# Tile 1's row numbers on their own, the largest expert as tile 10, and b2 added by rows outside the tiles

## The chip, the core and the metric

The kernel runs on one core of one Trainium2 chip. The metric is device time in microseconds of one execution, as the median of several. Times "at 320" are counted from the start of the profiled execution's span.

## The reference

The input is a table x of 625 rows (tokens) by 512, with 20,000 edges. Four residual layers follow one another: a graph convolution, a small feed-forward layer on a few features, a three-layer graph network, and last a tree-routed mixture of 16 experts. Only the last one is touched here. In short:

```
leaf = 4 binary decisions of a router on the normed rows      # one of 16 experts for each row
for each expert (w1 512x2048, b1, w2 2048x512, b2), m = (leaf == expert):
    h = gelu(xn @ w1 + b1)
    out += m * (h @ w2 + b2)
result = x + out
```

All weights are float32: 4 MB for w1 and 4 MB for w2 of each expert. With these inputs the largest expert has 73 rows, the others 16 to 54, 625 in all.

## The kernel before

The layers ahead of the experts run until about 290 us. The rows before the last layer (x3) are then stored into `out`, and their normed form into a table `normed_rows` in DRAM; both in five chunks of 125 rows.

The expert layer works by tiles. A tile is up to 64 rows of one expert (SA), and one tile, called "more" in the code, has 32 further rows (SB_) for the expert with the most rows. Tiles go in pairs: tile i = 2p + b uses buffer b of w1_sb, w2_sb, xT, y_sb. There are 16 tiles here (the pair count `last` is 7, read from the device). Experts 0, 1 and 2 are always tiles 0, 1 and 2, so that their weights can be fetched before the router has run; the largest of the other experts is exchanged with whichever expert would stand at tile `last2`, the first of the last pair (tile 14 here).

For one tile, TensorE (PE) multiplies the turned rows by w1 into two PSUM banks (32 matmuls, `first_a`, L952), turns each bank (L969), adds a product of a one-hot column with the b2 rows (2 matmuls of 256 columns by two halves, L986: this starts the accumulation), turns the rows of the next tile (`turn_rows`, L908), and multiplies the gelu of the hidden rows by w2 (64 matmuls, `second_a`, L1000). The more-tile adds `first_b` (L961) and `second_b` (L1012) for its 32 further rows. DVE copies banks (L1392), turned rows (L1318) and the tile's bias column (L1394); ScalarE does gelu (L629) and copies the result to y_sb (L641).

GpSimd moves rows by indirect DMA on the software queue: `gather` brings the rows of a tile from normed_rows into x_row (L458), `scatter` adds a tile's result to `out` (L466), both with row numbers that `pick` copies (L452). A number that stands for an empty slot is over the bound and is skipped. In its loop GpSimd, for tile i, waits until the rows of tile i+1 are turned, gathers tile i+2, scatters tile i, and waits until that has landed. There is one x_row, so a gather can't start before the rows ahead of it are turned. Ahead of the loop it gathers tile 1 and the more-tile's 32 rows.

The order of the start: tile 0's rows don't come by gather but by a product of a selector with the normed rows (L914, L1314). The row numbers of all tiles after it are worked out in `number_rows` on DVE (L1364 to L1384) during tile 0, with a product on PE in its midst (`slot_tokens`, L927). Only then (s_idx) does GpSimd gather tile 1. PE turns tile 1's rows after tile 0's last product.

SyncE (SP) issues the weight loads, 2 MB each (two halves of w1, L378, and two of w2, L386), on the hardware queue, in a fixed order: w1 of tile 4 once tile 0 has used its buffer, w2 of tile 2, w1 of tile 3, w2 of tile 3, w2 of tile 4, w1 of tile 5, w2 of tile 5, and then w1 and w2 of tile i+2 with tile i. Each half waits for PE to have used the same half of that buffer (s_w1u, s_h, s_l2). The first 16 MB are fetched long before.

Of the kernel before, what the change touches and what calls it, by code (L numbers as in the profile page):

```python
# [62 lines left out]
FIXED = 3  # L63
MORE = (N_NODES - 1) // SA
# [6 lines left out]
def build(nc, x, src, dst, Wconv, bconv, Wlin, blin, Wa, ba, Ws, bs, Wg, bg, Wr, br, W1, b1, W2, b2, out):  # L71
    ctx = ExitStack()
    with ctx:
# [117 lines left out]
        row_inB = row_inB[0:2 * SB_, :]  # L191
        half_ofB = maps[:, 950:951]
# [5 lines left out]

        b1T = FB[:, 1536:1536 + NE * (MH + 1)].rearrange("p (e m) -> p e m", e=NE)
        b1T_flat = FB[:, 1536:1536 + NE * (MH + 1)]  # L200
        bT = [FB[:, 1824 + b * (MH + 1):1824 + (b + 1) * (MH + 1)] for b in range(2)]

        w1_two = [G[:, 0:HID]] + [a[:, :, :].rearrange("p c n -> p (c n)")[:, 0:HID] for a in (C, xs, xn)]
        b2_rows = FB[:, 1900:1900 + DIM]
# [4 lines left out]
        def sv(at, *dims):  # L209
# [35 lines left out]
        s_sel = sem("tile0_selector_ready")  # L245
# [5 lines left out]
        s_b2, s_b1, s_b1T, s_b1Tc = (sem(n) for n in  # L251
            ("b2_in", "b1_in", "b1_transposed", "b1_copied"))
        s_b2z, s_xst, s_ost, s_slots, s_rows, s_idx = (sem(n) for n in
            ("b2_cleared", "normed_stored", "x3_stored", "slots_ready", "slot_rows", "row_numbers"))
        s_peh = sem("pe_held")
# [7 lines left out]
        s_xTB, s_xTBc, s_hB, s_hBc, s_hTB, s_geluB, s_l2B = (sem(n) for n in ("more_transposed",  # L263
            "more_copied", "more_hidden", "more_hidden_copied", "more_hidden_transposed", "more_gelu", "more_out"))
# [14 lines left out]
        def _(sp):  # L279
# [69 lines left out]
            sp.wait_ge(s_b2z, 1)  # L349
            sp.dma_start(b2_rows[0:NE, :], b2).then_inc(s_b2, 16)  # L350
# [52 lines left out]
        def _(pool):  # L403
# [34 lines left out]
            pool.wait_ge(s_gh, NCH * 3)  # L438
            nc.gpsimd.memset(b2_rows, 0.0).then_inc(s_b2z, 1)
            pool.sem_inc(s_yfree, 2)  # L440
            pool.wait_ge(s_xst, 16 * 2 * NCH)
            pool.wait_ge(s_table, 1)
            last = pool.value_load(npairs_t[0:1, 0:1], min_val=NE // 2 - 1, max_val=MAX_PAIRS - 1)
            pool.wait_ge(s_idx, 3)

# [23 lines left out]

            pool.wait_ge(s_xT, 1)  # L470
            gather(1, 1)
            pick(row_inB, 2, 2 * last, 2)
# [4 lines left out]
            pool.wait_ge(s_ost, 16 * 2 * NCH)  # L477
            with pool.Fori(0, last) as p:
                for b in range(2):
                    i = 2 * p + b  # L480
                    hold(s_xT, i + 2)
                    gather(i + 2, 2 * i + 3)
                    scatter(i, b, 2 * i + 4)
                    hold(s_yst[b], 16 * p + 16)
                    pool.sem_inc(s_yfree, 1)
            scatter(2 * last, 0, 4 * last + 3)
            pick(row_outB, 1, 2 * last, 4 * last + 4)
            pool.wait_ge(s_ycpB, 1)
            nc.gpsimd.indirect_dma_start(out=out.rearrange("t (g n) -> (t g) n", g=4),
                                         out_offset=bass.IndirectOffsetOnAxis(ap=row_outB, axis=0), in_=y_sbB, in_offset=None,  # L490
                                         bounds_check=4 * N_NODES - 1, oob_is_err=False, compute_op=ALU.add).then_inc(s_ystB, 16)
            scatter(2 * last + 1, 1, 4 * last + 5)
# [6 lines left out]
        def _(act):  # L499
# [120 lines left out]
            def tile_out(p, b, end=False):  # L620

                i = 2 * p + b
                more = end and b == 0
# [18 lines left out]
                if more:  # L642
                    act.wait_ge(s_l2B, 1)
                    nc.scalar.activation(y_sbB, P[:, 5, 0:128], ACT.Copy).then_inc(s_ycpB, 1)

            with act.Fori(0, last) as p:
                for b in range(2):
                    tile_out(p, b)
            for b in range(2):
                tile_out(last, b, end=True)  # L650
# [3 lines left out]
        def _(pe):  # L654
# [264 lines left out]
            pe.wait_ge(s_b2z, 1)  # L919
            pe.wait_ge(s_b2, 16)  # L920
# [10 lines left out]
            def tile(p, b, end=False):  # L931

                i = 2 * p + b
                more = end and b == 0
# [7 lines left out]
                def first_ready(j):  # L942
                    if not usual:
                        pe.wait_ge(s_w1_two, 16 * KD)
                    elif b or isinstance(p, int):
                        pe.wait_ge(s_w1[b][j], 16 * (p + 1))
                    else:
                        pe.wait_ge(s_w1[b][j], 16 * p)

                def first_a(h, k):  # L950
# [3 lines left out]
                    if k == KD - 1:  # L954
                        mm.then_inc(s_h, 1)
                    elif h == 1 and k == 1:
                        mm.then_inc(s_w1u, 1)

                def first_b(k):
# [3 lines left out]
                    if k == KD - 1:  # L963
                        mm.then_inc(s_hB, 1)

# [5 lines left out]

                for j in range(2):
                    first_ready(j)
                    for h in range(2):
                        for k in (2 * j, 2 * j + 1):
                            first_a(h, k)
                if more:
                    pe.wait_ge(s_xTBc, 1)
                    for k in range(KD):
                        first_b(k)  # L980
# [13 lines left out]
                def second_a(q):  # L994
# [3 lines left out]
                    for m in range(4 * q, 4 * q + 4):  # L998
                        for g in range(2):
                            mm = nc.tensor.matmul(P[g * SA:(g + 1) * SA, 7, 0:256], hT[:, m, :], w2_sb[b][:, m, g * 256:(g + 1) * 256],  # L1000
                                                  start=False, stop=(m == MH - 1))
                    mm.then_inc(s_l2, 1)

                def second_b(q):
                    pe.wait_ge(s_geluB, q + 1)
                    if q == 0:
                        for g in range(4):
                            nc.tensor.matmul(P[g * SB_:(g + 1) * SB_, 5, 0:128], bT[b][:, MH:MH + 1].to_broadcast([128, SB_]),
                                             b2_rows[:, g * 128:(g + 1) * 128], start=True, stop=False)
                    for m in range(4 * q, 4 * q + 4):  # L1010
                        for g in range(4):
                            mm = nc.tensor.matmul(P[g * SB_:(g + 1) * SB_, 5, 0:128], hTB[:, m, :], w2_sb[b][:, m, g * 128:(g + 1) * 128],  # L1012
                                                  start=False, stop=(m == MH - 1))
                    return mm

                second_a(0)
                if more:
                    pe.wait_ge(s_hBc, 1)
                    turn(0, 2).then_inc(s_hTB, 1)
                for q in range(1, 4):  # L1020
# [6 lines left out]
                if more:  # L1027
                    for q in range(4):
                        mm = second_b(q)
                    mm.then_inc(s_l2B, 1)  # L1030
# [6 lines left out]
            with pe.Fori(2, last) as p:  # L1037
# [3 lines left out]
            pe.wait_ge(s_hc, 4 * last)  # L1041
            pe.sem_inc(s_peh, 1)
# [4 lines left out]
            for b in range(2):  # L1047
                tile(last, b, end=True)

        @block.vector  # L1050
        def _(dve):
# [212 lines left out]
            for d in range(4):  # L1264
# [16 lines left out]
            more, last2, tmp = small[:, 744:750], small[:, 750:751], small[:, 752:756]  # L1281
            ts(thr[:, :], iota[:, 0:16], float(SA), None, ALU.mult)
            rank, not0, rank0 = sv(0, NCH, NE), sv(90, NCH), sv(100, NCH)
            link(ts(not0[0:NC, :], leaf[0:NC, :, 0], -EMPTY, EMPTY, ALU.mult, ALU.add))
# [3 lines left out]
            link(tt(rank0[0:NC, :], rank[0:NC, :, 0], not0[0:NC, :], ALU.add))  # L1288
            tt(sel[0:NC], iota[0:NC, 0:SA].unsqueeze(1).to_broadcast([NC, NCH, SA]),
               rank0[0:NC, :].unsqueeze(2).to_broadcast([NC, NCH, SA]), ALU.is_equal).then_inc(s_sel, 1)  # L1290
# [25 lines left out]
            def copy_inputs(i, b):  # L1316
# [9 lines left out]
            link(ts(last2, more[:, 5:6], 2.0, float(NE - 2), ALU.mult, ALU.add))  # L1326
            copy_inputs(0, 0)
            link(tt(top[:, :], big[:, :], iota[:, 0:NE], ALU.mult))
# [8 lines left out]
            link(ts(at2, iota[:, 0:TAB + 2], last2, None, ALU.is_equal))  # L1337
            ts(one, iota[:, 0:TAB + 2], tmp[:, 0:1], None, ALU.is_equal)
            link(tt(row, eid, at2, ALU.mult))
            link(nc.vector.tensor_reduce(tmp[:, 1:2], row, AX.X, ALU.add))  # L1340

            link(tt(one, one, at2, ALU.subtract))
            tt(tmp[:, 2:3], tmp[:, 1:2], tmp[:, 0:1], ALU.subtract)
            link(tt(tmp[:, 3:4], last2, tmp[:, 0:1], ALU.subtract))
            link(stt(pos, one, tmp[:, 3:4], iota[:, 0:TAB + 2], ALU.mult, ALU.add))
            link(stt(eidf, one, tmp[:, 2:3], eid, ALU.mult, ALU.add))
# [8 lines left out]
            nc.vector.tensor_copy(b1T[:, :, 0:MH].rearrange("p e (q r) -> p e q r", r=8),  # L1355
                                  P[:, 5, 0:256].rearrange("p (r e q) -> p e q r", r=8, q=2))
            nc.vector.tensor_copy(b1T[:, :, MH], ident[:, 0:NE]).then_inc(s_b1Tc, 1)
# [28 lines left out]
            def tile_copies(p, b, end=False):  # L1386
# [3 lines left out]
                for t in range(2):  # L1390
                    dve.wait_ge(s_h, 2 * i + t + 1)
                    nc.vector.tensor_copy(h_sb[:, t, :].rearrange("p (r n) -> p r n", r=4), P[:, t, :].rearrange("p (n r) -> p r n", r=4)).then_inc(s_hc, 1)  # L1392
                    if t == 0:
                        nc.vector.tensor_copy(bT[b], b1T_flat[:, bass.ds(e * (MH + 1), MH + 1)]).then_inc(s_bTc, 1)  # L1394
                if end and b == 0:
# [4 lines left out]
                if not (end and b):  # L1400
# [36 lines left out]
```

## Time and profile before

| what | value |
|---|---|
| median of 3 runs | 613.92 us (612.63 to 615.91) |
| the profiled execution | 611.82 us, span 609.9 us |
| PE busy | 532.0 us (87%) |
| DVE, ScalarE, GpSimd busy | 191.5, 160.8, 62.4 us |
| moved by DMA | 145.71 MB, of which hardware queue 142.91 |
| granted TensorE clock, mean | 0.983 |

PE is TensorE's matmuls, PEld its weight loads, ACT ScalarE, POOL GpSimd, SP the engine that issues the weight loads. A group of the profile names the line, engine, operation, output<-input, and at its end, behind the bar, busy time and mean ns of one, and then the idle time before it with what ended most of it. "DMA to landing" is the time from the issue instruction's start to the last byte.

### The profile page before, as it was taken

How to read it: one execution, taken by the hardware profiler on the slowest of the kernel's cores; microseconds unless marked ns; L12 is line 12 of the kernel's file. 1: busy time of each engine (PE TensorE's matmuls, PEld its weight loads, DVE VectorE, ACT ScalarE, POOL GpSimd, SP SyncE). 2: the span in 40 equal slices, each digit the busy share in tenths (PEclk: the TensorE clock that was granted, in tenths of full speed). 3: DMA queues.
4: the chain of work that ended last, by engine and by line, in shares of the span. 5: the costliest groups of instructions: out<-in, count | busy, mean ns of one | idle time of the engine just before them, and what ended most of it. 6: DMA issues, size and time to landing. Idle time of an engine off the chain costs nothing.

```text
span 609.9 us, 9957 instructions
## 1 busy us (share of the span) xinstructions
PE 532.0 (87%) x3090; PEld 284.6 (47%) x3090; DVE 191.5 (31%) x600; ACT 160.8 (26%) x548; POOL 62.4 (10%) x88
## 2 busy tenths in 40 slices
PE   1967878889899999999895999999998778878994
PEld 1534555544356657444451555555543344334463
DVE  5997777482520010146740101111111001100100
ACT  1667778202011101002120222222222022202311
POOL 3000000021000000000012221221112120212021
PEclk9979999999999999999897999999999999999998
DMA  6169900100202010024686979999999999999980
GB/s 122 13 223 429 429 21 5 30 0 0 87 1 70 0 36 33 0 89 140 226 352 253 420 304 423 421 426 421 424 425 420 422 428 425 421 422 432 418 338 7
DMA packets 25209, 145.71 MB, mean 239 GB/s; under 512 B 10335, under 2 KB 12585, under 8 KB 16738
## 3 DMA queue, kind: packets, MB, share of 16 engines
q1 hardware_dynamic: 21986, 142.91, 57.9%
q0 software_dynamic: 3200, 2.50, 2.0%
q8 instruction: 14, 0.23, 0.1%
q14 instruction: 9, 0.07, 0.0%
HBM read 142.38 MB, written 4.72 MB: 241 GB/s over the span
## 4 chain that ended last, share of the span: by engine, by line
PE 58%; DMA 20%; DVE 8%; ACT 6%; issue 5%; ACTq 2%; POOL 0%; DVEq 0%; SPq 0%; POOLq 0%
DMA w<-in_L_ffn_W 18%; PE P L952 13%; PE P L1000 11%; PE P L839 8%; PE P L849 7%; PE P L858 4%; ACT H L537 2%; PE P L693 2%; ACT H L543 2%; PE P L969 2%; DVE stats L1134 2%; DMA XT<-normed_rows,C 1%; PE P L986 1%; PE P L802 1%; PE P L801 1%
## 5 line engine op out<-in xcount | busy, mean ns | idle before, releaser
L952 PE MATMUL P<-w,H 128*64 128x512 f32 x480 | 108.6, 600 | 17.1 <-DMA w<-in_L_ffn_W 15.8
L1000 PE MATMUL P<-w,FB 128*64 128x256 f32 x1024 | 115.6, 381 | 5.5 <-DMA w<-in_L_ffn_W 5.5
L629 ACT ACTIVATE FB<-P,FB 128x64 f32<-128x64 f32 x256 | 54.3, 362 | 156.2 <-PE P L969 156.2
L1000 PEld LDWEIGHTS P<-w,FB 128*64 128x64 f32 x1024 | 72.0, 137 | 43.9 <-issue 10.7
L1392 DVE COPY H<-P 128x512 f32<-128x512 f32 x32 | 22.1, 692 | 215.2 <-PE P L952 215.2
L693 PE MATMUL P<-H 125*125 125x500 bf16 x176 | 59.6, 414 | 18.5 <-ACT H L543 18.0
L952 PEld LDWEIGHTS P<-w,H 128*64 128x64 f32 x480 | 35.9, 138 | 81.6 <-issue 60.5
L1116 DVE TENSOR_SCALAR H<-iota,small 125x626 bf16<-125x626 f16 x176 | 60.2, 382 | 14.0 <-issue 8.9
L839 PE MATMUL P<-G,XT 128*125 128x512 f32 x120 | 52.0, 592 | 0.0
L693 PEld LDWEIGHTS P<-H 125*125 125x125 bf16 x176 | 25.1, 143 | 44.5 <-ACT H L543 30.9
L849 PE MATMUL P<-C,H 125*128 125x313 f32 (+1 forms) x160 | 42.4, 425 | 0.0
L694 PE MATMUL P<-H 125*125 125x127 bf16 x176 | 40.0, 227 | 0.0
L1234 DVE TENSOR_SCALAR H<-P,dis_c 125x512 f32<-125x512 f32 x15 | 11.3, 751 | 83.8 <-PE P L839 83.8
L537 ACT ACTIVATE H<-iota,small 125x126 bf16<-125x126 f16 x88 | 30.4, 392 | 23.6 <-issue 15.0
L849 PEld LDWEIGHTS P<-C,H 125*128 125x128 f32 x160 | 30.2, 189 | 12.5 <-issue 1.0
L839 PEld LDWEIGHTS P<-G,XT 128*125 128x125 f32 x120 | 22.4, 187 | 27.9 <-issue 27.6
L466 POOL DMA_INDIRECT out<-XT,C x16 | 25.6, 1602 | 79.8 <-ACT XT L641 78.7
L543 ACT ACTIVATE H<-H,ones 125x126 bf16<-125x126 bf16 x88 | 30.6, 392 | 5.4
L641 ACT ACTIVATE XT<-P 128x256 f32<-128x256 f32 x16 | 6.2, 384 | 87.2 <-PE P L1000 87.2
L452 POOL COPY C<-C 128x1 int32 (+2 forms) x33 | 7.4, 225 | 194.4 <-DMA out<-XT,C 130.0
L605 ACT ACTIVATE XT<-P,bg_c 128x313 f32<-128x313 f32 (+1 forms) x16 | 8.4, 523 | 67.9 <-PE P L849 67.9
L694 PEld LDWEIGHTS P<-H 125*125 125x125 bf16 x176 | 25.6, 145 | 0.0
(294 smaller groups left out, 441.9 us busy)
## 6 DMA issues: line engine op xcount, KB each, us to landing
w<-in_L_ffn_W SPq DMA_DIRECT2D x62, 2048.0 KB, 28.7
G<-in_L_gnn_W SPq DMA_DIRECT2D x3, 1024.0 KB, 5.3
xs<-in_x SPq DMA_DIRECT2D x1, 1120.0 KB
out<-xs SPq DMA_DIRECT2D x5, 224.0 KB
normed_rows<-xn SPq DMA_DIRECT2D x5, 224.0 KB
G<-in_L_ffn_W SPq DMA_DIRECT2D x1, 1024.0 KB, 5.0
C<-in_L_ffn_W SPq DMA_DIRECT2D x1, 1024.0 KB, 5.3
xs<-in_L_ffn_W SPq DMA_DIRECT2D x1, 1024.0 KB, 7.3
```

What stands on the lines that cost most here:

```text
L466: nc.gpsimd.indirect_dma_start(out=out.rearrange("t (g n) -> (t g) n", g=2), out_offset=bass.IndirectOffsetOnAxis(ap=row_out[b], axis=0), ...
L537: near = nc.scalar.activation(sqd[0:NC, j, :], iota[0:NC, even:even + DW], ACT.Square, bias=ef[0:NC, 1, j, bass.ds(lo_g + u, 1)], scale=-1.0)
L543: nc.scalar.activation(D[0:NC, j, :], sqd[0:NC, j, :], ACT.Relu, bias=ones[0:NC, 0:1], scale=-1.0).then_inc(s_dhot, 1)
L629: g = nc.scalar.activation(hT[:, m, :], P[:, 3 + rd, c * SA:(c + 1) * SA], ACT.Gelu, bias=bT[b][:, m:m + 1])
L693: nc.tensor.matmul(P[0:NC, b0, 0:GROUP], hot, S[0:NC, j, 0:GROUP], start=False, stop=False, skip_group_check=True)
L694: nc.tensor.matmul(P[0:NC, b0 + 1, 0:LAST], hot, S[0:NC, j, GROUP:GROUP + LAST], start=False, stop=False, skip_group_check=True).then_inc( ...
L839: mm = nc.tensor.matmul(P[0:NC, c, :], XTn[:, k, c * NC:(c + 1) * NC], Gw[:, k, :], start=(k == 0), stop=(k == KD - 1))
L849: mm = nc.tensor.matmul(P[:, (5 + g) % 8, 0:b - a], Hn[0:NC, c, m * 128:(m + 1) * 128], C[0:NC, c, a:b], start=(c == 0), stop=(c == NCH - 1))
L858: mm = nc.tensor.matmul(P[0:NC, (5 + t) % 8, :], C[0:NC, c, t * NC:(t + 1) * NC], Hn[0:NC, c, :], start=(c == 0), stop=(c == NCH - 1))
L952: mm = nc.tensor.matmul(P[g * SA:(g + 1) * SA, h, :], xT[b][:, k, :], w1a[k][:, h, g], start=(k == 0), stop=(k == KD - 1))
L1000: mm = nc.tensor.matmul(P[g * SA:(g + 1) * SA, 7, 0:256], hT[:, m, :], w2_sb[b][:, m, g * 256:(g + 1) * 256], start=False, stop=(m == MH - 1))
L1116: hot = ts(S[0:NC, j, 0:NPAD], iota[0:NC, :], ef[0:NC, 0, j, bass.ds(lo_g + u, 1)], None, ALU.is_equal)
```

## The change

- DVE makes a selector for tile 1 (in `slots`) beside that of tile 0, and PE multiplies it with the token numbers (10 matmuls of one column). DVE turns that into tile 1's row numbers (`row_one`), which GpSimd uses for tile 1's gather without the numbers of all tiles. PE turns tile 1's rows before the last quarter of tile 0's second product.
- DVE also works out each token's expert (`expert_of`). GpSimd gathers, in five chunks of 125 tokens, that expert's row of b2, and adds these rows to `out` by five indirect DMAs. It waits for all five ahead of its loop over tiles.
- The load of the 16 rows of b2, its clearing, the one-hot column in the bias table and the products L986 (and those of the more-tile, L1008) go. The second product starts its own accumulation.
- The more-tile is tile 10 always (LARGE), not the first of the last pair. Its `first_b` is interleaved with `first_a`, and `second_b` with `second_a`; what releases its weight buffers is the last user of each part. The loops of all engines are split around tile 10.

```diff
+            link(tt(rank01[0:NC], rank[0:NC, :, 0:2], not01[0:NC], ALU.add))
...
+            tt(slots[0:NC], iota[0:NC, 0:SA].unsqueeze(1).to_broadcast([NC, NCH, SA]),
+               rank01[0:NC, :, 1:2].to_broadcast([NC, NCH, SA]), ALU.is_equal).then_inc(s_selx, 1)
+            link(tt(val[0:NC], leaf[0:NC], iota[0:NC, 0:NE].unsqueeze(1).to_broadcast([NC, NCH, NE]), ALU.mult))
+            link(nc.vector.tensor_reduce(not01.rearrange("p c t -> p (c t)")[0:NC, 0:NCH], val[0:NC], AX.X, ALU.add))
+            ts(row_of[0:NC, :], token[0:NC, :], -1.0, None, ALU.add)
+            nc.vector.tensor_copy(expert_of[0:NC, :], not01.rearrange("p c t -> p (c t)")[0:NC, 0:NCH]).then_inc(s_eid, 1)
...
+            dve.wait_ge(s_row1, 1)
+            v = P[:, 5, 384:385]
+            link(ts(row_one_f, v, 0.5, EMPTY, ALU.is_lt, ALU.mult))
+            link(stt(row_one_f, v, 2.0, row_one_f, ALU.mult, ALU.add))
+            tt(row_one, row_one_f, half_of, ALU.add).then_inc(s_idx1, 1)
```

GpSimd, ahead of its loop:

```diff
-            pool.wait_ge(s_xst, 16 * 2 * NCH)
-            pool.wait_ge(s_table, 1)
-            last = pool.value_load(...)
-            pool.wait_ge(s_idx, 3)
...
+            pool.wait_ge(s_ost, 16 * 2 * NCH)
+            pool.wait_ge(s_eid, 1)
+            for c in range(NCH):
+                nc.gpsimd.indirect_dma_start(out=b2_tok[c][0:NC, :], out_offset=None, in_=b2,
+                                             in_offset=bass.IndirectOffsetOnAxis(ap=expert_of[0:NC, c:c + 1], axis=0),
+                                             bounds_check=NE - 1, oob_is_err=False).then_inc(s_b2, 16)
+            pool.wait_ge(s_xst, 16 * 2 * NCH)
+            pool.wait_ge(s_xT, 1)
+            pool.wait_ge(s_idx1, 1)
+            nc.gpsimd.indirect_dma_start(out=x_row, ..., ap=row_one, ...).then_inc(s_xr, 16)
+            pool.wait_ge(s_b2, 16 * NCH)
+            for c in range(NCH):
+                nc.gpsimd.indirect_dma_start(out=out, out_offset=bass.IndirectOffsetOnAxis(ap=row_of[0:NC, c:c + 1], axis=0),
+                                             in_=b2_tok[c][0:NC, :], in_offset=None,
+                                             bounds_check=N_NODES - 1, oob_is_err=False, compute_op=ALU.add).then_inc(s_b2st, 16)
+            pool.wait_ge(s_table, 1)
+            last = pool.value_load(...)
+            pool.wait_ge(s_idx, 3)
+            pick(row_inB, 2, LARGE, 1)
+            pool.wait_ge(s_rowB, 1)
             nc.gpsimd.indirect_dma_start(out=x_rowB, ...).then_inc(s_xrB, 16)
+            pick(row_outB, 1, LARGE, 2)
+            pool.wait_ge(s_b2st, 16 * NCH)
+            pool.sem_inc(s_yfree, 1)
             ... loop: hold(s_xT, i + 2); gather(i + 2); scatter(i); hold(s_yst[b], 16 * p + 16)
```

PE, in a tile:

```diff
-                pe.wait_ge(s_bTc, i + 1)
-                pe.wait_ge(s_ycp, i + 1)
-                for g in range(2):
-                    nc.tensor.matmul(P[g * SA:(g + 1) * SA, 7, 0:256], bT[b][:, MH:MH + 1].to_broadcast([128, SA]),
-                                     b2_rows[:, g * 256:(g + 1) * 256], start=True, stop=False)
-                if not (first or end and b):
+                if not (first or end):
                     pe.wait_ge(s_xr, 16 * i + 16)
                     turn_rows(i + 1)
...
                 for q in range(1, 4):
                     if first and q == 2:
                         slot_tokens()
+                    if first and q == 3:
+                        pe.wait_ge(s_xr, 16)
+                        turn_rows(1)
                     second_a(q)
-                if first:
-                    pe.wait_ge(s_xr, 16)
-                    turn_rows(1)
```

## Rows read from the trace of the kernel before

**Rows 1.** Windows: busy of PE, PEld, DVE, ACT, POOL, clock, DMA share, GB/s.
```profile
307.00:327.00 20.00, 12.91 (x166) 8.19 (x162) 5.92 (x23) 3.78 (x17) 2.64 (x4) 0.90 1.00 411
328.00:332.00 4.00, 4.00 (x16) 1.18 (x14) 0.00 (x0) 0.00 (x0) 2.62 (x3) 0.77 0.08 23
355.00:360.00 5.00, 5.00 (x49) 3.31 (x47) 0.00 (x0) 0.73 (x4) 1.27 (x3) 1.00 0.40 105
360.00:592.00 232.00, 210.63 (x1530) 105.77 (x1528) 24.11 (x51) 48.96 (x222) 39.16 (x51) 1.00 1.01 421
```

**Rows 2.** Groups by line, 300 to 610 us: busy, mean ns, idle before.
```profile
L1000 PE MATMUL P<-w,FB 128*64 128x256 f32 x1024 | 115.6, 381 | 5.5 <-DMA w<-in_L_ffn_W 5.5
L466 POOL DMA_INDIRECT out<-XT,C x16 | 25.6, 1602 | 79.8 <-ACT XT L641 78.7 <-issue 1.1
L986 PE MATMUL P<-FB 128*64 128x256 f32 x64 | 10.4, 404 | 0.0
```

**Rows 3.** Chain of waits, tiles 14 and 15: start, us, what.
```profile
568.80 3.57 PE P L961 x32
...
582.56 3.49 PE P L1012 x128
...
595.02 7.08 PE P L1000 x64
...
603.37 1.57 POOL out L466
```

**Rows 4.** Timeline of PE around tile 1: start, us, instruction, wait before.
```profile
315.55 3.67 PE L1000 MATMUL P<-w,FB 128*64 128x256 f32 x32
326.32 0.70 PE L908 MATMUL P<-ident,XT 128*128 128x128 f32 x2 [7.09 <-DMA XT<-normed_rows,C]
327.54 8.21 PE L952 MATMUL P<-w,H 128*64 128x512 f32 x32 [0.52 <-DVE H L1318]
...
336.85 0.51 PE L908 MATMUL P<-ident,XT 128*128 128x128 f32 x2
```

**Rows 5.** Timeline of GpSimd in the same stretch.
```profile
317.64 0.18 POOL L452 COPY C<-C 128x1 int32<-128x1 int32 x1 [53.56 <-DVE C L1384]
318.83 1.26 POOL L458 DMA_INDIRECT XT<-normed_rows,C  x1 [1.00 <-POOL C L452]
...
328.31 1.05 POOL L458 DMA_INDIRECT XT<-normed_rows,C  x1 [0.85 <-POOL C L452]
```

**Rows 6.** Timeline of DVE ahead of tile 0.
```profile
294.92 0.49 DVE L1289 TENSOR_TENSOR XT<-iota,small 125x320 f32<-125x320 f16 x1
...
297.97 0.24 DVE L1307 TENSOR_TENSOR small<-small 125x80 f32<-125x80 f32 x1
```

**Rows 7.** Timeline of SP's weight loads.
```profile
306.24 2.79 SPq L378 DMA_DIRECT2D w<-in_L_ffn_W  x2
...
357.54 3.78 SPq L386 DMA_DIRECT2D w<-in_L_ffn_W  x2
```

**Rows 8.** Landings of the tile gathers, the scatters to out, and the last load.
```profile
DMA to landing us min/median/max: 2.6/6.8/7.9
...
DMA to landing us min/median/max: 3.3/10.8/12.1
...
L386 SPq DMA_DIRECT2D w<-in_L_ffn_W x1: 332/332/332, 559.1 to 559.1; - x1
...
DMA to landing us min/median/max: 36.7/36.7/36.7
```

**Rows 9.** DMA queues in 503 to 509.5 us, and in 605 to 607.5.
```profile
q1 hardware_dynamic: 188, 2.70, 97.9%
q0 software_dynamic: 144, 0.03, 4.1%
...
q0 software_dynamic: 144, 0.07, 28.6%
```

**Rows 10.** Window after PE's wait; columns as in rows 1.
```profile
326.00:329.00 3.00, 2.17 (x6) 0.85 (x8) 0.42 (x1) 0.00 (x0) 0.87 (x2) 0.50 0.59 242
```

More of the change, by code:

```diff
@@ L63 @@
 FIXED = 3
+LARGE = 10
 MORE = (N_NODES - 1) // SA
@@ L618, in _, with tile_out @@
             last = act.value_load(npairs_t[0:1, 0:1], min_val=NE // 2 - 1, max_val=MAX_PAIRS - 1)
-            def tile_out(p, b, end=False):
+            def tile_out(p, b):
                 i = 2 * p + b
-                more = end and b == 0
+                more = isinstance(p, int) and i == LARGE
                 act.wait_ge(s_bTc, i + 1)
@@ L649, in _ @@
             for b in range(2):
-                tile_out(last, b, end=True)
+                tile_out(LARGE // 2, b)
+            with act.Fori(LARGE // 2 + 1, last) as p:
+                for b in range(2):
+                    tile_out(p, b)
+            for b in range(2):
+                tile_out(last, b)
         @block.tensor
@@ L933, in tile @@
                 i = 2 * p + b
-                more = end and b == 0
+                more = isinstance(p, int) and i == LARGE
                 first = isinstance(p, int) and i == 0
@@ L955, in first_a @@
                         mm.then_inc(s_h, 1)
-                    elif h == 1 and k == 1:
+                    elif h == 1 and k == 1 and not more:
                         mm.then_inc(s_w1u, 1)
@@ L1000, in second_a @@
                             mm = nc.tensor.matmul(P[g * SA:(g + 1) * SA, 7, 0:256], hT[:, m, :], w2_sb[b][:, m, g * 256:(g + 1) * 256],
-                                                  start=False, stop=(m == MH - 1))
-                    mm.then_inc(s_l2, 1)
+                                                  start=(m == 0), stop=(m == MH - 1))
+                    if not more:
+                        mm.then_inc(s_l2, 1)
                 def second_b(q):
                     pe.wait_ge(s_geluB, q + 1)
[L1006 to L1009, printed above, removed]
                     for m in range(4 * q, 4 * q + 4):
@@ L1047, in _ @@
             for b in range(2):
-                tile(last, b, end=True)
+                tile(LARGE // 2, b)
+            with pe.Fori(LARGE // 2 + 1, last) as p:
+                for b in range(2):
+                    tile(p, b)
+            for b in range(2):
+                tile(last, b, end=(b == 1))
         @block.vector
@@ L1399, in tile_copies @@
                     number_rows()
-                if not (end and b):
+                if not end:
                     copy_inputs(i + 1, 1 - b)
@@ L1404, in _ @@
                 tile_copies(0, b)
-            with dve.Fori(1, last) as p:
+            with dve.Fori(1, LARGE // 2) as p:
                 for b in range(2):
@@ L1411, in _ @@
             for b in range(2):
-                tile_copies(last, b, end=True)
+                tile_copies(LARGE // 2, b)
+            with dve.Fori(LARGE // 2 + 1, last) as p:
+                for b in range(2):
+                    tile_copies(p, b)
+            for b in range(2):
+                tile_copies(last, b, end=(b == 1))
 _INS = ["x", "src", "dst", "L0_gnn_W_conv", "L0_gnn_b_conv", "L0_gnn_W_lin", "L0_gnn_b_lin", "L0_ffn_Wa", "L0_ffn_ba",
```

164 lines of the change are left out of this document (89 added, 75 removed).

## The prediction

> **What bounds the kernel now.** I read the stage windows first [rows 1]. From 360 to 592 us the DMA engines are full (share 1.01, 421 GB/s), and just before there are two holes: 328 to 332 us (share 0.08) and 355 to 360 us (0.40). From the windows the two holes are worth about 9 us of transfer time: 4 x 0.92 + 5 x 0.60 = 6.7 us, and some 2.5 us more at their edges (the first runs from about 327.5 to 333). TensorE has work for 211 of the 232 us of the full stage, so there a faster PE gives nothing; the expert weights bound it. The groups by line [rows 2] say what the tiles cost; the chain of waits [rows 3] says what comes last. The first hole has a cause that can be named: tile 0 ends on PE at 319.2, the next PE work is the turning of tile 1's rows at 326.32 after 7.09 us of waiting on the gather from normed_rows [rows 4], and that gather was issued only after the row numbers of all tiles (317.64 and on) [rows 5]. The second hole follows from it: tile 4's second-layer weights are issued at 357.54 [rows 7], when tile 2's product has used half of that buffer, and the loads in between are done by then.
>
> The last load is issued at 559.1 and lands 36.7 us later [rows 8], at 595.8. PE is not ready for it: tile 14 has spent 3.57 us on the larger expert's first layer and 3.49 on its second [rows 3], so tile 15's product runs from 595.02 to 602.10 and the load is no longer the last wait. If it were, the product's second half (3.6 us, half of the 7.08) would start at 595.8 and the kernel would end at 595.8 + 3.6 + 7.8 (from the end of PE's work to the end of the span, 602.1 to 609.9) = 607.2.
>
> **The change, part by part.**
>
> *Tile 1's numbers by themselves.* DVE gets, ahead of the row positions, a second selector like the 0.49 us one, a product and a sum over 125x80 like the 0.24 us one [rows 6], and two small instructions of about 0.15: 0.49 + 0.24 + 0.24 + 0.3 = 1.27 us. The chain that ends in tile 0's rows has no slack there, so tile 0 starts 1.2 us later. PE's ten one-column products stand where it waits for DVE: 0. In return the gather for tile 1 is issued near 304 instead of 318.8 and lands before 316 even at the loaded 7.9 us [rows 8]. Tile 0 on PE loses 0.58 (bias product) and gains 0.44 (the turn moves inside): it ends at about 319.2 + 1.2 - 0.6 + 0.5 = 320.3, and tile 1 starts there instead of at 327.54 [rows 4]. The first hole as it is now goes.
>
> *No product with b2 in the tiles.* 64 matmuls, 10.4 us [rows 2], 0.65 for each tile and 0.58 as they follow each other. In the full stage it hides beside the loads: worth 0. It counts where PE sets the pace, tiles 0 to 2: 0.6 each.
>
> *b2 by rows.* Five gathers and five adding scatters of 125 rows on GpSimd. The trace has none of 125 rows of 2 KB; the nearest rows are tile scatters of 128 rows. Below: if the engines were free, each would take 1.6 us to issue, and its 144 packets 28.6% of 2.5 us, 0.7 us [rows 9]; five are down 8 + 3.3 = 11 us after they begin. Above: one behind the other at the loaded landing of 10.8 us [rows 8], 54 us. Which is nearer? In 6.5 us of the full stage, the software queue moved the 144 packets of one scatter (9 on each engine), and the hardware queue 188 packets, 2.70 MB; at 16 KB a packet that is 10 on each engine, 0.63 us apiece [rows 9]. It moved only 0.03 MB, so bytes aren't the price: every row, even an empty one, waits for one 16 KB packet of the weights. Five scatters are 5 x 9 = 45 turns an engine. With 0.63 for the weight packet and 0.1 for the row (0.7 us for nine unloaded packets), 45 x 0.73 = 33 us.
>
> When do they start? The expert numbers are ready at about 295.4 + 1.2 = 296.6 (tile 0's selector ends at 294.92 + 0.49). Five gathers with 1.05 to 1.3 us of issue each end near 303, tile 1's gather goes in between, b2's rows are in at about 305.5, and the first packets of the scatters move near 308. From 307.5 on the weights are queued without a break: tile 4's first layer at 307.4 (306.24 + 1.2 [rows 7]), tile 2's second at 315 and 320, tile 3's first at 324 and 327.5. These six loads are six times 5.15 us plus 5 us of the rows between, so they run to about 343. The scatters therefore stay loaded to their end: 308 + 33 = 341.
>
> *What waits for them.* GpSimd waits for all five before it enters its loop, and the first instruction there is tile 2's gather. Before, that gather is issued at 328.31, as soon as tile 1's rows are turned [rows 5]. Now it is issued at 341 + 1.1 (the number is copied, then the issue, as from 327.28 to 328.31 before) = 342.2, and lands in 2.6 us on an idle queue or up to 6.8 on a full one [rows 8]; the weights run out at about 343, so I take 3.8: 346. PE needs these rows in the middle of tile 1: it finishes tile 1's first layer at about 327.8 and then stands still for 18 us. Queued behind that wait on PE are tile 1's second turn and its product, whose steps release tile 3's second-layer loads, and then all of tile 2. Before, PE turned tile 2's rows at 336.85 [rows 4]; now at 346, 9.2 us later. PE also comes back at the low clock, as it does after the shorter wait (granted 0.50 from 326 to 329 [rows 10]); then it cost the first layer of tile 1 8.21 instead of 6.87 and the turn before it 0.2, which was over before 336.85. Now it comes behind that point: +1.6.
>
> *The weights after it.* The issue at 357.54 comes 20.7 us of PE work after the turn at 336.85. Now: 346 + 20.7 - 0.6 (b2 of tile 2) + 1.6 = 367.7, 10.2 us later. The engines have been dry from 343 until tile 3's second-layer load (near 352.5), and again before 367.7: two holes of 9.5 and 5 us in place of about 9 in sum. After this point the load is continuous as it was, 595.8 - 357.5 = 238.3 us to the last landing: 606.0.
>
> *Largest expert as tile 10.* Its 7.7 us of extra PE work (3.57, 3.49, a turn of 0.6) now falls in the full stage, where PE has some 4 us of slack in each tile's 20.5 and loads are issued 36 us before they land [rows 8]; the queue is never short of work: 0. At the end the last load is again the last wait: 606.0 + 3.6 + 7.8 = 617.4.
>
> **Sum.** 617.4 - 609.9 = +7.5 us on the profiled execution, whose own time is 611.82 (1.9 outside the span): 619.3. The median of the runs is 2.1 higher, 613.92; with it 621.4. I give 621.
>
> **Rivals.**
>
> *A, the b2 scatters are hidden.* If the software queue gets more than one row for each weight packet, or several at a time, they land before about 325, and PE never waits. For it: unloaded, nine packets take 0.7 us. Against: all loaded scatters take about 10.8 us. Then 54 loads run from 308.4 with no hole: the present 595.8 + 1.2 - 9 + 5 (rows of b2) = 593, end 593 + 11.4 = 604.4, so 606.3 profiled and 608.4 beside the median. Faster.
>
> *B, the same wait, but shorter.* The price is set by when tile 2's rows are there. The end is 617.4 + (that time - 346); no change is reached at about 338.5, and within 3 us from 335.5 to 341.5. GpSimd issuing sooner, or the last scatter finding the engines free, would do it: 613 to 615 beside the median.
>
> *C, 125 rows don't spread over all engines.* Nothing in this trace shows a transfer of 125 rows by GpSimd. If they went over five engines, 25 rows each, with the five transfers on different ones, the busiest would have 50 rows and gathers before them that land near 312; the scatters would begin at 313, still have some 5 rows at 346 when the weights run out, and end at 347: tile 2's rows at 351, +5, 626. All on the same five: 125 rows less 45 done, 80 x 0.15 = 12 us more, 638. The Trainium skill, DMA: Bandwidth & Descriptors, "Why a DMA increments its semaphore by 16 and not by 1", states such a rule: the split is by the largest number up to 16 that divides the outer size, which for 125 is 5, with an exception for some direct copies from GpSimd; no row here bears on it. By that rule, this rival.
>
> *D, the extra work at tile 10 starves the queue* and the last wait stays with PE: up to the 2.6 us of the tail not gained; inside the range.
>
> **Chances.** The forecast (tile 2's rows from 341.5 to 349.5) 0.50; C and later 0.17; B as no change 0.15; A and B so short that it is faster 0.18. A difference within 0.5% (3 us) can't be told from none: faster 0.18, same 0.15, slower 0.67. Range: the forecast's own is 617 to 625; down to 609, where most of A's side is left out, and up to 629 for C: 0.12 is left out below, 0.06 above.
>
> **What would show it.** Right: tile 1's first layer starts near 320 with no wait before it; the software queue is busy without a break from 308 to 341; PE then waits some 18 us on the gather in the middle of tile 1, ending near 346, with the granted clock at half after it; two holes in the DMA share near 345 to 352 and 363 to 368; from there 1.0 to the end; PE's last product waits for the last load. Wrong: PE's wait on that gather is under 10 us or absent, or the scatters are down before 330; or the last wait is not a load.

## The result and the profile after

The changed kernel takes 630.39 us in the median of four runs (629.97 to 631.78), against 614.22 for the kernel before (one run more than in the 613.92 above): 1.027 times the kernel before, 95% interval 1.023 to 1.030. It is slower, as forecast, but by 16 us and not by 7, and above the range of 609 to 629. The profiled execution took 629.97 us with a span of 628.2, 18.3 more than the 609.9 before.

First PE around tile 1 of the changed kernel, against [rows 4]. Columns: start, us, instruction, and in brackets the wait before it.

```profile
323.48 7.04 PE L985 MATMUL P<-w,H 128*64 128x512 f32 x32
330.45 0.66 PE L1004 MATMUL P<-ident,H 128*128 128x128 f32 x4
355.14 0.70 PE L937 MATMUL P<-ident,XT 128*128 128x128 f32 x2 [24.03 <-DMA XT<-normed_rows,C]
355.63 1.06 PE L1004 MATMUL P<-ident,H 128*128 128x128 f32 x4
```

The wait of 7.09 us before tile 1 is gone, and tile 1 begins 4 us earlier. In its place PE stands still for 24 us in the middle of tile 1, for tile 2's rows: turned at 336.85 before, at 355.14 now. GpSimd in the same stretch shows why (against [rows 5]):

```profile
298.16 1.49 POOL L468 DMA_INDIRECT H<-in_L_ffn_b,C  x1 [158.26 <-issue]
...
304.71 1.32 POOL L468 DMA_INDIRECT XT<-in_L_ffn_b,C  x1 [0.30 <-issue]
306.33 1.03 POOL L474 DMA_INDIRECT XT<-normed_rows,C  x1 [0.30 <-issue]
312.60 2.05 POOL L479 DMA_INDIRECT out<-H,C  x1 [5.23 <-DMA XT<-in_L_ffn_b,C]
...
321.93 2.00 POOL L479 DMA_INDIRECT out<-XT,C  x1 [0.30 <-issue]
...
351.37 0.18 POOL L446 COPY C<-C 128x1 int32 x1 [25.08 <-DMA out<-XT,C]
352.44 1.08 POOL L452 DMA_INDIRECT XT<-normed_rows,C  x1 [0.90 <-POOL C L446]
```

Line 468 (L468) holds the gathers of b2's rows, L474 is tile 1's gather (before: L458, 12.5 us later), L479 the adding scatters. The last of these has landed at 350.4 (issued at 321.93, 28.5 us to landing); GpSimd goes on at 351.37 and only then issues tile 2's gather.

The windows (columns as in [rows 1]) show two holes in the weight loads, from 346 to 361 and near 374 to 377, and the full stage after them, which is as it was:

```profile
344.00:348.00 4.00, 0.00 (x0) 0.00 (x0) 0.00 (x0) 0.00 (x0) 0.00 (x0) 0.50 0.77 173
348.00:352.00 4.00, 0.00 (x0) 0.00 (x0) 0.00 (x0) 0.00 (x0) 0.18 (x1) 0.50 0.21 36
352.00:356.00 4.00, 0.86 (x4) 0.87 (x5) 0.12 (x1) 0.00 (x0) 2.53 (x3) 0.50 0.06 14
356.00:360.00 4.00, 4.00 (x28) 2.38 (x28) 0.30 (x1) 1.75 (x8) 0.82 (x3) 0.70 0.18 19
360.00:364.00 4.00, 4.00 (x40) 2.59 (x38) 0.00 (x0) 0.00 (x0) 1.04 (x2) 1.00 0.53 142
...
372.00:376.00 4.00, 3.76 (x33) 2.84 (x34) 0.66 (x2) 3.39 (x16) 0.18 (x1) 1.00 0.34 103
...
400.00:600.00 200.00, 178.23 (x1314) 91.24 (x1310) 21.58 (x46) 44.66 (x204) 32.46 (x42) 1.00 1.01 422
```

Tile 4's second-layer weights, issued at 357.54 before [rows 7], now come 19.5 us later, and the chain of waits at its end has the last load in it, not PE's backlog as in [rows 3]. Below are two rows of SyncE's loads and then the end of the chain:

```profile
309.13 3.75 SPq L379 DMA_DIRECT2D w<-in_L_ffn_W  x2
...
377.04 3.78 SPq L387 DMA_DIRECT2D w<-in_L_ffn_W  x2
...
579.37 36.29 DMA w<-in_L_ffn_W
615.66 0.12 issue
615.78 3.69 PE P L1036 x32
```

### The profile page after: what moved, and what is told of

It reads as the page before. It is cut to its first block, busy times and chain, and to the rows that moved or that the text cites. A ratio compares the mean times of both kernels' runs of the same rounds, so it can differ in the third digit from the quotient of the medians.

```text
span 628.2 us, 9815 instructions
## 1 busy us (share of the span) xinstructions
PE 527.4 (84%) x3038; PEld 285.8 (45%) x3038; DVE 193.4 (31%) x603; ACT 160.9 (26%) x548; POOL 78.4 (12%) x96
## 4 chain that ended last, share of the span: by engine, by line
PE 51%; DMA 24%; ACT 8%; issue 6%; DVE 6%; ACTq 2%; POOL 2%; POOLq 0%; SPq 0%; DVEq 0%
DMA w<-in_L_ffn_W 17%; PE P L1036 12%; PE P L985 9%; PE P L868 8%; PE P L878 7%; DMA out<-XT,C 5%; PE P L887 3%; ACT H L568 3%; ACT H L562 3%; PE P L722 2%; DVE stats L1175 2%; DMA XT<-in_L_ffn_b,C 1%; ACT FB L654 1%; PE P L1004 1%; PE P L831 1%
## 5 line engine op out<-in xcount | busy, mean ns | idle before, releaser
L1036 PE MATMUL P<-w,FB 128*64 128x256 f32 x1024 | 117.1, 383 | 11.2 <-DMA w<-in_L_ffn_W 8.7
L1036 PEld LDWEIGHTS P<-w,FB 128*64 128x64 f32 x1024 | 75.6, 138 | 48.0 <-issue 13.2
L878 PEld LDWEIGHTS P<-C,H 125*128 125x128 f32 x160 | 30.2, 189 | 12.5 <-issue 1.0
L937 PE MATMUL P<-ident,XT 128*128 128x128 f32 x32 | 7.1, 307 | 26.2 <-DMA XT<-normed_rows,C 24.0
```

The source lines that it names most:

```text
L878: mm = nc.tensor.matmul(P[:, (5 + g) % 8, 0:b - a], Hn[0:NC, c, m * 128:(m + 1) * 128], C[0:NC, c, a:b], start=(c == 0), stop=(c == NCH - 1))
```

## The experiments

Below, "the changed kernel" is the one of 630.39 us. The runs of the kernel before beside the experiments had medians of 614.0, 613.3 and 612.7 us.

**e1: tile 2's gather ahead of the wait.** Cut to the moved lines:

```diff
-            pool.wait_ge(s_b2st, 16 * NCH)
-            pool.sem_inc(s_yfree, 1)
...
+            hold(s_xT, 2)
+            gather(2, 3)
+            pool.wait_ge(s_b2st, 16 * NCH)
+            pool.sem_inc(s_yfree, 1)
+            scatter(0, 0, 4)
```

> Only the order on GpSimd is changed: tile 2's gather is issued ahead of the wait for the five adding scatters of b2 (about 324 us instead of 352); only the first scatter of a tile's result waits for them. Theory of turns: the gather stands behind the 125 turns of the b2 scatters on the same software queue, so it lands with them, near 351, and PE gets tile 2's rows 3 to 4 us sooner than in the changed kernel (355.1): 626 to 627 us against 630.4. Rival, the wait on GpSimd is the cost and not the queue: the gather lands within 8 us, PE does not stand still, tile 4's second-layer load is issued near 352 instead of 377, and the time is about 606 us.

Measured: 627.5 us, ratio 1.022 (1.018 to 1.025). GpSimd and PE of this run:

```profile
328.20 1.08 POOL L452 DMA_INDIRECT XT<-normed_rows,C  x1 [1.28 <-issue]
...
351.24 0.70 PE L943 MATMUL P<-ident,XT 128*128 128x128 f32 x2 [20.11 <-DMA XT<-normed_rows,C]
```

Issued 24 us sooner, the gather landed 23.0 us after its issue, where a tile's gather takes 6.8 in the median [rows 8]. The order of the wait is worth 4 us of PE's wait and 3 us of time; the rest is the software queue, in which the gather stands behind the b2 scatters. The rival is out.

**e2: 128 rows instead of 125.**

```diff
-                nc.gpsimd.indirect_dma_start(out=b2_tok[c][0:NC, :], ..., ap=expert_of[0:NC, c:c + 1], ...
+                nc.gpsimd.indirect_dma_start(out=b2_tok[c][:, :], ..., ap=expert_of[:, c:c + 1], ...
...
-                nc.gpsimd.indirect_dma_start(out=out, ..., ap=row_of[0:NC, c:c + 1], ... in_=b2_tok[c][0:NC, :]
+                nc.gpsimd.indirect_dma_start(out=out, ..., ap=row_of[:, c:c + 1], ... in_=b2_tok[c][:, :]
+            link(nc.vector.memset(maps[:, 960:970].bitcast(I32), 8192))
```

> The b2 gathers and scatters have 128 rows instead of 125, with row numbers over the bound for the last three (skipped). Theory of turns: 125 has no larger divisor up to 16 than 5, so each scatter costs 25 turns on an engine; with 128 it costs 8 and one for the semaphore. The software queue then needs 45 x 0.73 = 33 us from about 308, the five scatters are down near 341, tile 2's rows are there near 346 instead of 355.1, and the time is 620 to 622 us. Some 720 packets in the software queue for the scatters instead of over 2000. Rival, the cost is in the bytes or the adding of 2 KB rows: no change, 630 us.

The memset puts a number over the bound into rows 125 to 127. (GpSimd also clears the last rows of the five buffers beforehand, not shown.)

Measured: 628.86 us, ratio 1.024 (1.021 to 1.027), where 620 to 622 was expected: a miss. The packets of the hardware queue (q1, the weights) and the software queue (q0), first in the changed kernel from 317 to 351, then here from 314 to 348, with the scatters under way (columns: packets, MB, share of the 16 engines' time):

```profile
q1 hardware_dynamic: 689, 9.98, 70.0%
q0 software_dynamic: 2112, 1.31, 23.0%
```

```profile
q1 hardware_dynamic: 793, 11.52, 81.0%
q0 software_dynamic: 752, 1.30, 20.6%
```

The number of packets fell as expected, 2112 to 752 for the same 1.3 MB, but the scatters took nearly the same time (37.6 us from the first issue to GpSimd's next step, 38.8 in the changed kernel). Narrower windows say why. The first pair is this run from 316 to 346, the second the changed kernel from 328 to 344, and the last line the changed kernel from 344 to 351:

```profile
q1 hardware_dynamic: 698, 10.11, 80.6%
q0 software_dynamic: 699, 1.24, 22.2%
...
q1 hardware_dynamic: 390, 5.77, 85.6%
q0 software_dynamic: 387, 0.50, 17.2%
...
q0 software_dynamic: 1099, 0.49, 43.6%
```

In these windows the software queue moves one packet for each of the weights', be it a row or a few bytes (from 342 to 344 it is 52 against 52, with 0.00 MB). In the changed kernel two short stretches fall out, 320 to 322 with 363 against 60 and 326 to 328 with 133 against 42; why isn't shown. With 128 rows the scatters end that way, after 752 such packets. With 125 rows about half of the 2112 packets are still waiting at 344, and they go in the last 6 us, because the weights run out. So it is by accident that the two times are alike. PE had tile 2's rows at 351.09, 4 us sooner; 2.9 of them because the b2 gathers landed sooner. The profiled execution is 2.8 us shorter, the medians only 1.5. GpSimd and PE:

```profile
309.70 1.62 POOL L482 DMA_INDIRECT out<-H,C  x1 [3.44 <-DMA XT<-in_L_ffn_b,C]
...
347.27 0.18 POOL L446 COPY C<-C 128x1 int32 x1 [22.60 <-DMA out<-XT,C]
...
351.09 0.70 PE L940 MATMUL P<-ident,XT 128*128 128x128 f32 x2 [19.11 <-DMA XT<-normed_rows,C]
```

**e3: the weight loads wait for the scatters.** One line on SP:

```diff
+            sp.wait_ge(s_b2st, 16 * NCH)
             load_w1(4, 0, user=0)
```

> The weight loads of the expert stage (from tile 4's first layer on) wait until the b2 scatters have landed. Theory of turns: without weight packets in between the scatters are bound by their issue, 5 x 2.3 us from 312.6, and are down near 326; the loads start there, 17 us later than in the changed kernel, but have no hole after it: 54 loads take 279 us as before, last landing near 606, time 619 to 621 us, so the kernel that starts its loads 17 us later is about 10 us faster. Rival, the scatters are slow by themselves (2 KB rows, read and added in DRAM): they still take until 345 to 350, the loads start then, and the time is over 640 us.

Measured: 629.86 us, ratio 1.025 (1.022 to 1.028). It is neither theory's number: 619 to 621 was expected, and over 640 by the rival. GpSimd and SP:

```profile
311.90 2.05 POOL L480 DMA_INDIRECT out<-H,C  x1 [4.93 <-DMA XT<-in_L_ffn_b,C]
...
336.03 0.18 POOL L447 COPY C<-C 128x1 int32 x1 [10.24 <-DMA out<-XT,C]
```

```profile
335.90 0.88 SPq L379 DMA_DIRECT2D w<-in_L_ffn_W  x2
```

Without weights beside them the scatters take 24.1 us instead of 38.8: the weights are part of their time, but not all. The other half of the theory held: the loads begin 27 us later than in the changed kernel, have no hole after it (share 1.01 from 340 to 600), 54 loads take 279 us from first issue to last landing, and the kernel is no slower.

**e5: both edits.**

> Both edits at once: b2's gathers and scatters of 128 rows, and the weight loads held until the scatters have landed. With 125 rows and held weights the scatters took 20 us of transfer, about 4 us each, which is not the turns with the weights. Theory: 125 rows lie on few engines at a time (25 rows of 0.2 us one after the other, and small packets on the others), 128 rows on all 16 (8 each). Then the five are bound by GpSimd's issue, 1.9 us each, and are down near 321 instead of 336; loads start near 322, last landing 322 + 279 = 601, time 613 to 616 us. Rival, adding 625 rows of 2 KB in DRAM takes 20 us however they are spread: down near 330, time 622 us or more.

Measured: 620.96 us, ratio 1.013 (1.008 to 1.018). The first scatter, GpSimd going on, and the first load:

```profile
310.47 1.62 POOL L483 DMA_INDIRECT out<-H,C  x1 [3.66 <-DMA XT<-in_L_ffn_b,C]
...
324.45 0.18 POOL L447 COPY C<-C 128x1 int32 x1 [0.68 <-DMA out<-XT,C]
```

```profile
324.72 0.88 SPq L379 DMA_DIRECT2D w<-in_L_ffn_W  x2
```

The four runs make a table, from the first scatter's issue to GpSimd's next step:

| | weights beside | weights held |
|---|---|---|
| 125 rows | 38.8 us | 24.1 us |
| 128 rows | 37.6 us | 14.0 us |

Alone, 128 rows save 10 us, and what is left is mostly issue (five of 1.9 us). From 314 to 318, with the first scatters under way, the software queue looks like this, first with 125 rows (e3), then with 128 (e5), both without weights:

```profile
q0 software_dynamic: 359, 0.15, 33.5%
...
q0 software_dynamic: 262, 0.46, 98.7%
```

With 125 rows the packets keep a third of the 16 engines busy, as if some 5 were at work (later, with several scatters in flight, 63.9% from 318 to 326); with 128 rows all of them. With weights beside, the two rows of the table are alike only because the weights run out (e2). The time was 5 us above the top of what I expected: the scatters ended 3 us later, the last load landed at 604.1 instead of 601, and the median is 2.3 us above the profiled execution.

**e4: no b2 at all.** The gathers, the scatters and their waits are taken out.

> The b2 gathers and scatters and the waits for them are left out (the result lacks b2); all else as in the changed kernel. Theory of turns: all of the loss is theirs. Tile 1 starts near 321 and PE does not wait in it; 54 loads from 310 without a hole worth more than 1 to 2 us take 279 us, last landing 590, time 603 to 605 us. Rival, part of the loss is in the other edits (tile 0 later, largest expert as tile 10): 610 us or more.

Measured: 607.16 us, ratio 0.988 (0.985 to 0.992). The b2 transfers cost 23 us, more than the whole loss; the rest of the change gains 7. PE has tile 2's rows 21 us sooner than in the changed kernel:

```profile
333.87 0.50 PE L927 MATMUL P<-ident,XT 128*128 128x128 f32 x2 [1.93 <-DMA XT<-normed_rows,C]
```

The time is 2 to 4 us over the expectation, since 54 loads took 283 us from the first issue at 309.95, not 279.

**e6: b2 in the tiles as before, the rest of the change kept.**

```diff
-            (gathers and scatters of b2, expert numbers on DVE)
+                pe.wait_ge(s_bTc, i + 1)
+                pe.wait_ge(s_ycp, i + 1)
+                for g in range(2):
+                    nc.tensor.matmul(P[g * SA:(g + 1) * SA, 7, 0:256], bT[b][:, MH:MH + 1].to_broadcast([128, SA]),
+                                     b2_rows[:, g * 256:(g + 1) * 256], start=True, stop=False)
```

> The changed kernel with b2 as it was before (a product in each tile, no rows of b2 gathered or scattered, no expert numbers on DVE); tile 1's own numbers and tile 10 stay. Theory: the product of 0.58 us a tile is hidden beside the loads, so this is as fast as the kernel without any b2 (607.2), or 1 us faster since DVE's chain ahead of the weight table is 0.8 us shorter: 605 to 608 us. Rival, the product costs PE time that counts: 607 + 16 x 0.58 = 616 us.

Measured: 604.96 us, ratio 0.987 (0.981 to 0.992). The product with b2, 10.4 us of PE [rows 2], costs nothing that can be measured: this is 2 us faster than e4, which has no b2 at all, with a first load 2.7 us earlier. SP's first load and the chain's end:

```profile
307.28 3.75 SPq L381 DMA_DIRECT2D w<-in_L_ffn_W  x2
```

```profile
553.99 36.26 DMA w<-in_L_ffn_W
...
590.37 3.69 PE P L1035 x32
```

This version is 1.3% faster than the kernel before, and faster than the changed one.

**e8: the move of the largest expert alone.**

```diff
-            pick(row_inB, 2, 2 * last, 2)
+            pick(row_inB, 2, LARGE, 2)
...
-                more = end and b == 0
+                more = isinstance(p, int) and i == LARGE
```

> The kernel before with one part of the change alone: the largest expert is tile 10, not 14; b2 in the tiles, tile 1's numbers with all others as before. Theory: the two holes stay, the last load lands at 595.8 as before, and the last product now waits for it: end 607.3 to 608, time 609.5 to 610.5 us. Rival, the last wait is not a load but PE's own backlog: 614 us, no change.

Measured: 612.5 us, ratio 0.998 (0.995 to 1.001): no change that can be told, and above the 609.5 to 610.5 expected. In the trace the last product does wait for the last load, as expected:

```profile
327.09 0.70 PE L926 MATMUL P<-ident,XT 128*128 128x128 f32 x2 [7.51 <-DMA XT<-normed_rows,C]
```

```profile
560.92 36.23 DMA w<-in_L_ffn_W
...
597.26 3.69 PE P L1026 x32
```

but tile 1's gather was 0.8 us later than in the kernel before, the last load landed at 597.1 instead of 595.8, and the span is 608.8 against 609.9.

**e10: tile 1's own numbers alone.**

```diff
+            pool.wait_ge(s_idx1, 1)
+            nc.gpsimd.indirect_dma_start(out=x_row, ..., ap=row_one, ...).then_inc(s_xr, 16)
             (before: gather(1, 1) behind pool.wait_ge(s_idx, 3))
...
+                    if first and q == 3:
+                        pe.wait_ge(s_xr, 16)
+                        turn_rows(1)
```

> The kernel before with one part of the change alone: tile 1's own numbers and its rows turned inside tile 0; b2 in the tiles, the largest expert still as tile 14. Theory: the first hole goes, last landing 590 to 591 instead of 595.8 as in the kernel with b2 in the tiles (e6), but PE then has the larger tile at the end and the last product does not wait for that load; tile 14 can start 5 us earlier than before, so the end is 5 us earlier, 604.5 to 605.5, time 606.5 to 608.5 us; the move to tile 10 is worth the rest to e6 (605.0). Rival, without the move PE's backlog at the end eats the gain: 612 us or more.

Measured: 607.41 us, ratio 0.989 (0.985 to 0.993), as expected. So this part carries most of the gain (1.1% of the 1.3% in e6). PE is the last wait again: the last load lands at 592.0, three microseconds before the second half of the last product, which needs it, would begin:

```profile
591.54 7.08 PE P L1010 x64
```

Its span is 606.5 against 601.9 with the move as well (e6), but 1.6 us of that is a later first load; the medians, 607.4 and 605.0, have intervals that overlap, so the worth of the move on top isn't settled.

**e7 and e9: the start.** In e7 tile 1's selector comes after the table of experts:

```diff
             nc.vector.tensor_copy(tab[0:1, :], eidf[0:1, :]).then_inc(s_table, 1)
+            tt(slots[0:NC], iota[0:NC, 0:SA]..., rank01[0:NC, :, 1:2]..., ALU.is_equal).then_inc(s_selx, 1)
```

> As the kernel with b2 in the tiles and tile 1's own numbers, but tile 1's selector and numbers are worked out on DVE after the table of experts, and multiplied on PE in the middle of tile 0's first layer, so that nothing is added ahead of tile 0 and of the first weight load. Theory: the load stage is 54 loads of 279 us and begins when the table is there, so each us of DVE work ahead of it costs one at the end: first load at 306.0 as before instead of 309 to 310, last landing 586 to 587, time 600 to 602 us. Rival, the start is hidden by something later (a hole at tile 4's second-layer load): no faster than the kernel with the selector early, 605 to 607.

Measured: 606.8 us, ratio 0.989 (0.986 to 0.993); no better than e6, and not the 600 to 602 expected. DVE's table was there at 304.54, as early as in the kernel before, but PE was slow:

```profile
300.67 0.50 PE L929 MATMUL P<-ident,XT 128*128 128x128 f32 x2 [2.26 <-DVE XT L1361]
301.89 5.35 PE L981 MATMUL P<-w,H 128*64 128x512 f32 x16 [0.72 <-DVE H L1365]
```

```profile
307.44 4.34 SPq L381 DMA_DIRECT2D w<-in_L_ffn_W  x2
```

Sixteen products at the full level take 3.65 us (e9 below); here 5.35. The buffer's release, and with it the first load, waited for them. I put this down to the 2.26 us of idle time before. e9 fills it:

```diff
             mm.then_inc(s_xrow, 1)
+            pe.wait_ge(s_w2[0][0], 16)
+            keep_warm(4, w2_sb[0][0:NC, 0, :], bank=2)
             pe.wait_ge(s_xrowc, 1)
```

> As the kernel with tile 1's selector later (e7), with four idle products of 512 columns on PE between tile 0's selector product and the turn of its rows, where e7's PE is idle for 2.26 us and comes back at the low clock (tile 0's first 16 products took 5.35 us). Theory: PE keeps the full level, tile 0's first half is 1.8 us shorter, so the buffer's release and the first weight load come at 305.8 to 306.2 instead of 307.4, and as the load stage has no hole after it the end comes 1.2 to 1.6 us earlier: 603 to 605 us against e7's 604 to 607. Rival, the first load waits for the table of experts and not for PE: no change.

Measured: 607.53 us, ratio 0.990 (0.986 to 0.994). A miss, the expectation was 603 to 605:

```profile
299.49 4.07 PE L679 MATMUL P<-w,ident 125*128 125x512 f32 x8
...
304.51 3.65 PE L983 MATMUL P<-w,H 128*64 128x512 f32 x16 [0.72 <-DVE H L1367]
```

Four such products take 4.07 us, not the 2.26 that were idle, so tile 0 began 2.6 us later than in e7, and the first load came at 308.74, 1.3 us later. Two might do it; that wasn't tried. Tile 0's products are at the full level here (3.65 us). That the added products kept it there isn't shown. The windows of e7 from 302 to 305 and of e9 from 297 to 300 (columns as in [rows 1]):

```profile
302.00:305.00 3.00, 3.00 (x8) 1.04 (x9) 2.69 (x12) 0.00 (x0) 0.00 (x0) 0.50 0.22 90
...
297.00:300.00 3.00, 3.00 (x13) 1.50 (x12) 2.62 (x12) 0.00 (x0) 0.00 (x0) 0.50 0.04 16
```

Both executions have a stretch at half clock. In e7 it follows PE's idle time, which itself was at 1.00, and falls into tile 0; in e9 it begins earlier, in tile 0's selector product, and the clock is back at 1.00 from 301 on. In the kernel before it lies from 296 to 299, also ahead of tile 0, without any added products.

## Why the prediction was right or wrong

*Direction and place: right.* The wait goes from before tile 1 to its middle, it is tile 2's gather behind the b2 scatters, PE returns at the low clock (granted 0.50 from 352 to 356), two holes open in the loads, and the end is again a load. e4 shows that all of the loss is b2's, and e1 that the queue, not only GpSimd's wait, holds the gather.

*The step that failed is when the scatters start to move.* The prediction had b2's rows in at about 305.5 and the first packets of the scatters at 308; they were in at 312.5, and the first packets moved at 317.6. So tile 2's rows were there at 355.1, not at 346. The rest of the sum, taken from the rows of before, held: from the turn of tile 2's rows to tile 4's load 21.9 us (forecast 21.7), from that issue to the last landing 238.6 (238.3), from there to the end 12.5 (11.4). Those make 0.2 + 0.3 + 1.1, and with 9.1 the 10.7 us that were missing in the profiled execution (forecast 619.3, measured 629.97). The median lies only 0.4 above that execution, not 2.1, so the forecast of 621 misses it by 9.4. The 9.1 us are:

- b2's rows were in 7.1 us late. The gathers began 1.6 us later, each took 1.58 us or more from issue to issue instead of up to 1.3 (1.5 us in sum), and the last was down 6.5 us after the end of its issue, not 2.5. With 128 rows the gathers are down 2.9 us sooner (e2); the rest would have been missed with them too, and why those still land 4.7 us after the last issue isn't shown.
- From there to the first packet it took 5.0 us instead of 2.5, +2.5. With the weights held it took 2.6 (e3).
- From the first packet to the last landing, at 350.4, it took 32.8 us where 33 were forecast, -0.2. This agreement is luck, as the next paragraph says.
- GpSimd's next steps and the gather took 4.7 us instead of 5, -0.3.

*One row for each weight packet.* For 128 rows this holds: 33 us were worked out from nine turns for each scatter, and in e2 the packets moved from 314.5 to 346.8, 32 us, one for one with the weights' (699 and 698). Taking the weights away takes off 23.6 us (e2 to e5). For 125 rows the turns hold too from 328 to 344 (387 and 390), but their number was wrong: 2112 packets, about 26 an engine and scatter where nine were assumed. At that pace they would have needed some 96 us (an estimate: 132 packets an engine at the prediction's 0.73 us). They did not, since GpSimd's wait stops PE and PE stops the loads: the last weights go at 346, and about half of the packets go from 344 on with little or nothing beside them. 125 rows are also slow by themselves (24.1 us against 14.0 without weights).

*Rival C was the nearest,* with the gathers down near 312 (312.5), 351 for tile 2's rows (355.1) and 626 us; I gave it 0.17. The runs bear it out: 125 rows make 2112 packets for the five scatters and 128 make 752, 125 rows keep a third of the engines busy where 128 keep all (e3, e5), and 10 us lie between them when nothing else runs. The rule of the Trainium skill named beside it (DMA: Bandwidth & Descriptors, "Why a DMA increments its semaphore by 16 and not by 1") fits these numbers; which engines the rows went to can't be read here. As to the time, the even spread that I assumed in its place cost 1.2 us in the scatters and 2.9 in the gathers (e2), nearly half of the 9.1.

*Tile 10, worth the tail:* nothing that can be told alone (e8: 0.8 us in the medians, 1.1 in the spans), where the forecast counted on 2.7. *b2's product, worth 0 in the full stage:* right (e6). *Tile 0, 1.2 us later:* it was 2.0, and its first layer took 8.96 us instead of 7.09 (granted 0.50 from 303 to 307, where it was 1.00 before); covered here by the longer wait, but in e6, e7 and e10, where that layer is slow as well, the first load comes 1 to 3 us later than before. One reading was loose: a gather beside full queues lands after up to 7.9 us, 6.8 is the median [rows 8]; the sum used 3.8 and doesn't change.

## What to carry to other kernels

Before moving small work from an idle-looking engine to a queue of transfers, count the queue's turns beside the large packets that share it, and ask what stands behind it: here 10 us of hidden products were traded for 38 us in the one queue that brings every tile its rows. Count packets, not bytes or rows: 125 rows made nearly three times as many as 128. A wait for "all of it" ahead of a loop is a barrier for everything that the loop issues first. And the part of the change that was worth having, one small gather freed from a long computation of numbers, gave its 5 us only with the b2 transfers out of its way.

## What the runs showed of the hardware

- An adding scatter of 625 rows of 2 KB in five pieces, from the first issue to GpSimd's next step: 14.0 us without weights with 128 rows a piece (e5), 24.1 with 125 (e3). Beside 16 KB weight packets 37.6 us with 128 rows (e2); with 125 rows 38.8, of which the last 5 were without weights.
- 128 rows a piece made 752 packets and took 98.7% of the 16 engines' time from 314 to 318; 125 rows made 2112 packets and took 33.5% of it (e5, e3, both without weights).
- Beside the weights, the software and the hardware queue moved as many packets as each other: 699 and 698 in 30 us (e2), 387 and 390 in 16 us (the changed kernel from 328 to 344), though those of the one hold 2 KB or a few bytes and those of the other 16 KB.
- A gather behind those scatters on the same software queue landed after 23.0 us instead of 6.8 (e1).
- In e7 the granted clock was at its lower level (0.50, 1.2 GHz) from 302 to 305, after PE had been idle for 2.26 us, and tile 0's 16 products took 5.35 us; at the full level they took 3.65 (e9).
- GpSimd's issue costs 1.6 us for an adding scatter of 128 rows (e2) and 2.0 for one of 125; for a gather of b2's rows 1.0 and 1.3, and 0.2 to 0.4 more for the first of five.
